# A Mamba and expert layer in eight chunks: the product for B and C as four blocks of 128 tokens in four groups of 32 output rows of one bank

## The reference

```
xn      = rmsnorm(layernorm(x)) * rms_w
xs, res = split(xn @ W_in)                       # 512 channels each
xs      = silu(conv4(xs) + conv_b)
dt, B, C = split(xs @ W_x, [512, 528])           # B and C: 16 values a token each
dt      = softplus(dt @ W_dt)
h[t]    = exp(-exp(A_log) * dt) * h[t-1] + dt * B[t] * xs    # 16 states a channel
y[t]    = sum over states of h[t] * C[t]
x       = x + layernorm(x) + (y * silu(res)) @ W_out
out     = x + expert(layernorm(x))               # 8 experts, 512 tokens each
```

## Time and profile before

| | |
|---|---|
| times of three runs | 986.39, 986.48 and 990.32 us (median 986.48) |
| span of the profiled execution, first to last instruction | 989.0 us |
| busy: POOL, DVE | 891.3 us (90%), 900.1 us (91%) |
| busy: ACT | 731.6 us (74%) |
| chain that ended last | PE 37%, DVE 36%, ACT 15%, issue 11% |
| DMA | 117 GB/s over the span |

### The profile page before, as it was taken

One profiled execution on the slowest core, in us unless ns is written; L12 is line 12 of the kernel. 1 busy time (PEld: TensorE's weight loads), 2 busy tenths in 40 slices (PEclk: granted clock), 3 DMA queues, 4 the chain that ended last, 5 costly groups with the idle time before them and its releaser, 6 DMA issues.

```text
span 989.0 us, 13017 instructions
## 1 busy us (share of the span) xinstructions
PE 922.8 (93%) x4172; PEld 601.7 (61%) x4172; DVE 900.1 (91%) x966; ACT 731.6 (74%) x1305; POOL 891.3 (90%) x424
## 2 busy tenths in 40 slices
PE   6998998999999999999999999999999998769898
PEld 4555455655866566755756557655767556755765
DVE  5789899899999999999999999999999989999951
ACT  4566877888779877888788887888788786567530
POOL 0388899999999999999999999999999999999920
PEclk9898999999999999999999999999999999679899
DMA  5490136011651038111571037210580127200110
GB/s 174 173 343 22 43 134 252 1 67 59 247 209 45 23 115 351 49 67 43 195 276 43 25 102 299 114 67 0 187 327 3 44 75 290 107 22 1 61 50 21
DMA packets 43476, 116.82 MB, mean 118 GB/s; under 512 B 8592, under 2 KB 27024, under 8 KB 34192
## 3 DMA queue, kind: packets, MB, share of 16 engines
q1 hardware_dynamic: 41552, 115.94, 31.5%
q10 hardware_dynamic: 1856, 0.04, 0.1%
HBM read 110.21 MB, written 5.77 MB: 117 GB/s over the span
## 4 chain that ended last, share of the span: by engine, by line
PE 37%; DVE 36%; ACT 15%; issue 11%; DMA 1%; DVEq 0%; SPq 0%; ACTq 0%
DVE ring L657 25%; PE gbank L1090 19%; DVE ring L642 9%; PE ybank L1153 7%; PE gbank L1104 7%; ACT ebank L786 4%; ACT hb L1019 2%; ACT sres L867 1%; ACT xs L863 1%; PE gbank L1098 1%; ACT L1015 1%; ACT L875 1%; ACT L871 1%; DMA hb<-in_L_attn_W_x_dram 1%; PE gbank L1224 1%
## 5 line engine op out<-in xcount | busy, mean ns | idle before, releaser
L657 DVE TENSOR_TENSOR_SCAN ring<-ebank,state,ring 128x512 f32<-128x512 f32 x512 | 623.5, 1266 | 32.7 <-ACT ebank L786 25.7
L515 POOL TENSOR_TENSOR hc<-ring,c_all 128x1024 f32<-128x1024 f32 x255 | 598.8, 2364 | 17.4 <-DVE ring L657 9.6
L786 ACT ACTIVATE ebank<-dt_,a_neg 128x512 f32<-128x512 f32 x512 | 347.0, 689 | 163.2 <-DVE ring L657 160.6
L1153 PEld LDWEIGHTS ybank<-ident,hc 128*128 128x128 f32 x2048 | 240.2, 145 | 102.9 <-issue 53.1
L1153 PE MATMUL ybank<-ident,hc 128*128 128x128 f32 x2048 | 267.7, 280 | 28.3 <-POOL hc L515 19.6
L501 POOL TENSOR_TENSOR ring<-b_all,u 128x1024 f32<-128x1024 f32 x109 | 257.9, 2366 | 10.5 <-DVE taken L606 9.5
L642 DVE TENSOR_TENSOR ring<-b_all,ubank 128x1024 f32<-128x1024 f32 x145 | 173.1, 1194 | 0.0
L1090 PE MATMUL gbank<-xT,w 128*128 128x512 f32 x320 | 148.9, 599 | 14.7 <-DVE hb L737 11.9
L1090 PE MATMUL gbank<-xT,w_a 128*128 128x512 f32 x256 | 120.2, 606 | 8.0 <-DVE dt_ L631 4.4
L1090 PEld LDWEIGHTS gbank<-xT,w 128*128 128x128 f32 x320 | 57.7, 191 | 82.1 <-issue 57.1
L1090 PE MATMUL gbank<-xs,w_a 128*128 128x512 f32 x224 | 100.8, 593 | 0.7 <-ACT sres L804 0.7
(11 more groups left out here) (145 smaller groups left out, 777.1 us busy)
## 6 DMA issues: line engine op xcount, KB each, us to landing
b_all<-bc_kept SPq DMA_DIRECT2D x32, 1024.0 KB, 6.6
c_all<-bc_kept SPq DMA_DIRECT2D x32, 1024.0 KB, 8.4
w<-in_L_ffn_w_dram SPq DMA_DIRECT2D x16, 640.0 KB, 4.8
w_a<-in_L_attn_W_in_dram SPq DMA_DIRECT2D x7, 1024.0 KB, 4.9
w_a<-wc_kept SPq DMA_DIRECT2D x7, 1024.0 KB, 4.8
w2s<-in_L_ffn_w_dram SPq DMA_DIRECT2D x8, 640.0 KB, 9.3
xin<-in_L_attn_x_dram SPq DMA_DIRECT2D x9, 512.0 KB, 3.5
x<-in_L_attn_x_dram SPq DMA_DIRECT2D x7, 512.0 KB, 6.4
```

What stands on the lines that cost most here:

```text
L515: ch_ok.by(e.tensor_tensor(hc[:, q % HC, :, :], ring[:, q % RING, :, :], c_all[:, n:n + NG, :], ALU.mult))
L657: h_ok.by(e.tensor_tensor_scan(row, ebank[j % 2][:, :], row, initial=state[:, q, n:n + 1], op0=ALU.mult, op1=ALU.add))
L786: e_ok.by(e.activation(ebank[j % 2][:, :], dt_[:, d, :], ACT.Exp, scale=a_neg[:, d, k:k + 1]))
L1153: last = e.matmul(ybank[:, cols(b)], hc[:, q % HC, n, cols(b)], ident[:, :], is_transpose=True, start=(k == 0 and n == 0 and b == 0), stop ...
```

## The change

For the chunks 1 to 7 the product for B and C is cut by tokens: each of the four blocks of 128 tokens has its own 32 partitions of the bank (block b: partitions 32b to 32b+31, columns 0 to 127). PE issues 16 products of 128 columns, for each block of channels four, one for each group of output rows, where it issued 4 of 512 columns. ACT copies 128 x 128 values to the first quarter of `yt`, where it copied 32 x 512 to `hb`. The transfer to `bc_kept` reads 128 partitions of 512 bytes, where it read 32 of 2,048 bytes, and puts them in the same places in memory.

Since `yt` also carries y, the waits change. `bc_read` waits until PE has read `yt` for YT 0 (in iteration 0: YT 1), and no longer for the transfer of the chunk before; `y_read` of the next block (1, in iteration 0: 2) waits until the transfer to `bc_kept` has landed.

```diff
+        bc_b = yt[:, 0:P]
+        BC_AFTER = (1, 0)
...
-                    e.dma_start(bc_kept[:, :], bc_s).then_inc(bc_out.sem, 16)
+                    e.dma_start(bc_kept[:, :].rearrange("m (b t) -> b m t", b=NT), bc_b).then_inc(bc_out.sem, 16)
...
             def bc_read(c, i):
-                bc_out.wait(e, c - 1)
                 bank = wait_full(e, i, "BC", 0)
-                read_out(e.activation(bc_s, bank[0:W, :], ACT.Copy), i, "BC", 0)
+                if c == 0:
+                    read_out(e.activation(bc_s, bank[0:W, :], ACT.Copy), i, "BC", 0)
+                else:
+                    wait_full(e, i, "YT", BC_AFTER[i > 0])
+                    read_out(e.activation(bc_b, bank[:, 0:P], ACT.Copy), i, "BC", 0)
 
             def y_read(d):
                 def job(c, i):
 
                     y_ok.wait(e, c, GPD * (d + 1))
+                    if has_front(i) and d == BC_AFTER[i > 0] + 1:
+                        bc_out.wait(e, c + 1)
...
-                filled(product(bank[0:W, :], [(wbc[:, k, :], xs[:, k, :]) for k in range(ND)]), i, "BC", 0)
+                for k in range(ND):
+                    for b in range(NT):
+                        last = e.matmul(bank[b * W:(b + 1) * W, 0:P], wbc[:, k, :], xs[:, k, cols(b)], start=(k == 0), stop=(k == ND - 1),
+                                        skip_group_check=True)
+                filled(last, i, "BC", 0)
```

## The result

The changed kernel took 991.68 us (median of 10 runs, 990.79 to 995.34), the kernel before 988.35 (10 runs, 986.39 to 990.34). The ratio is 1.0041, with a 95% interval of 1.0027 to 1.0054: about 4 us slower (the means of the ten runs lie 4.0 us apart, the medians 3.3), just inside the 0.5% that the prediction called no change, and clear of zero. The median of before was 986.48 in its first three runs; with the more runs that follow it lay between 987.4 and 988.4. Every ratio is taken from undisturbed executions; it leaves out one of the kernel before that took 1094.86 us at a mean granted clock of 0.841.

The account below looks back on a forecast made before the run. An iteration was taken as bound first by DVE with pieces of ACT, then mostly by PE; the product lies in DVE's half. Every term summed to 0 in seven chunks, giving 986.5 us, range 984 to 996.5.

Parts of the forecast that it names:

- the forecast's sum: Whole kernel: product, copy and waits each add 0 in each of seven chunks, so the median stays 986.5 us.
- PE's clock falls: First rival, at transposes behind OXT: 2.2 us gap halves PE's clock, 1.3 us a chunk, 996 in all; chance 0.10 + 0.10.
- a clock of 0.50 behind the transposes: Sign of being wrong: PE's granted clock at 0.50 behind the transposes at 320.50 in iterations 1 to 6.
- The step that gave 1.8: Product for B and C on PE: taken as 1.8 us, leaving PE about 2.2 us ahead of the transposes at 320.50.
- The waits, the copy and the transfer: ACT's copy, its added waits and the transfer in 128 pieces: each 0, hidden behind waits for DVE or later use.
- Changing the output group costs: Rival, product on PE: 15 group changes at 0.12 us each make it 5.4 us, total 995; chance 0.10, far end 0.02.
- The time saved arrives: Rival: PE's saved 1.8 us goes through at POOL's product or the bank at 332.23, 7 x 1.8, so 974; chance 0.07.
- The cover of 0.74 us: PE's waits for POOL before the transposes and for ACT's bank at 332.23, 0.43 + 0.31 us, to spare each iteration.

Follow-up runs that it names:

- waits_only: The kernel before's four products of 512 columns, with the changed kernel's place in `yt`, waits and transfer (32 partitions of 2,048 bytes): 1.0001 to the kernel before.
- fill_all: The changed kernel with the whole product for B and C made four times over in chunks 1 to 7: 1.0004 to the kernel before.
- fill_rest: The changed kernel with the product for B and C four times over in iterations 1 to 6, once in iteration 0: 1.0038 to the kernel before.
- dt0_pe: The changed kernel with product DT 0 moved one group earlier on PE alone, behind OXT; ACT and DVE keep their order: 1.003 to the kernel before.
- fill_8: The changed kernel with the product for B and C made eight times over in chunks 1 to 7: 1.0177 to the kernel before.
- fill_first: The changed kernel with the product for B and C four times over in iteration 0 alone: 1.0016 to the kernel before.

## Why the prediction was right, and where it was not

What it forecast as likeliest, no change that can be told by 0.5%, is what came, and the time lies in its range. The time is 5.2 us above the likeliest value of 986.5; 1.9 of that is the median of before, which rose from 986.48 to 988.35 with more runs, and the other 3.3 are the change's. They are clear of the noise: the true case is the forecast's sum together with its first rival. One of the prediction's own signs of being wrong appeared, a clock of 0.50 behind the transposes in iteration 3. The time lies in the range because its top, 996.5, was set to hold this rival in all chunks.

The sum of the parts held. The product became shorter (1.08 us, near the lower bound of 0.9 rather than the 1.8 to 3.7 that I took), and not a bit of it reached the end: with the clock up, iterations take 113.15 us in all kernels with this order of jobs on ACT and DVE that have the product between 1.08 and 3.70 us. The step that gave 1.8 was wrong. It let only two groups run side by side, because the two records of a product share a group; the trace has the records start in sets of four. How the two records of each product are placed among them, no row names.

The waits, the copy and the transfer held, each at 0, by waits_only and fill_all. In iteration 0 the copy waited for YT 1 as worked out, and the next decay still waited for DVE.

The rival "PE's clock falls" is what the loss is made of. It was given 0.20, half of it for losses too small to be told; its mechanism was right and its place was not. It was priced at one place, the transposes behind OXT in iterations 1 to 6, at a gap of 2.2 us and 1.3 us a fall, and this price was taken for all seven chunks. There a fall costs 1.1 us, but a step was missed: OXT must wait for its banks until ACT has read RES, so the gap is parted in two of 1.2 us, and the wait for POOL grew by 0.8 us and not by all that the product lost. The clock fell in only some iterations (one of six in the changed kernel's trace). And iteration 0 was not looked at for itself. Its wait of 0.69 us was used as cover, but not as what the saved time would be added to: 0.69 + 2.51 = 3.20 us in front of DT 0, which stands on the chain of waits. It lost 2.8 us there in the trace, and fill_rest, with the product short in that iteration alone, lost 3.8 (its trace shows 3.4).

"Changing the output group costs" fell: 15 changes fit in 1.08 us. "The time saved arrives" fell: no iteration became shorter, and with dt0_pe the wait moves on and stays. The cover of 0.74 us was too small by 0.5, by fill_8, without effect on the forecast.

## What to carry to other kernels

A shorter product on an engine that then waits is not free: before shortening TensorE's work off the path, add the time saved to each wait behind it, and look at what runs after the longest sum; if that is on the path, a fall of the clock turns the saving into a loss. Read this for the odd iteration too, the first one here, not only for the one that repeats. Where nothing useful fits the gap, repeating the product kept the clock up at that place at no cost that can be told (fill_all, 1.0004).

## What the runs showed of the hardware

Four float32 products of 32 output rows, in four different 32-row groups of a bank and next to each other in the queue, ran 3.4 times as fast as one after another (1.08 us against 3.70 for as many records of full width); with each group's products in a row it was 1.5 times (2.46 us). Made eight times over, a product took 7.20 / 8 = 0.90 us, four times as fast: what a single product takes beyond that is paid once, however often it is repeated. The Trainium skill (TensorE: Matmul & The Clock Gate, Part 3) gives 2.38 times for three groups, and the trace agrees in kind.

Two waits of PE of 1.2 us with 1 us of transposes between were at times enough to bring the granted clock to 0.50 (iteration 3 of the changed kernel, iteration 2 of fill_first), though each is shorter than the wait of 1.79 us that the kernel before has in every iteration at full clock.

The length of a wait doesn't decide alone: behind 2.17 us in iteration 0 the clock held in the kernel before and fell in fill_all.

The times of each kernel that was run ten times or more spread over some 4 us or more. The setup shows where much of it can be: its length up to the first marked product was 113.9 to 118.6 us in executions that do the same work up to there. Effects of 0.1% can't be read from single runs of this kernel, but they can be read from the starts of a repeated instruction.
